# Summing the two feature halves of x2 on GpSimd ahead of the down projection's product with ones, with new stage orders on all engines

## The reference, cut to what matters

```
L0: x1 = x  + x @ W(entry) + bias(entry)             # W(entry) = U(entry) @ V, rank 30, U decoded from cond
L1: x2 = x1 + clip(((x1*style) @ weight.T)*dcoef + bias, -256, 256)
L2: w_down = down_project*dg + db                     # dg, db: one number per entry and hidden unit
    down = x2 @ w_down ; act = relu(down)
    w_up = up_project*ug + ub ; x3 = x2 + x2 + act @ w_up
L3: h, t, s = layernorms of x3 with gathered gains; m, n, r = x3 + small nets
    y = LN( silu(cat(h,t,m,n,r,s) @ W1 + b1) @ W2 + b2 ) ; out = x3 + y
```

## Time and profile before

| | |
|---|---|
| median of the runs | 519.8 us |
| span of the profiled execution, first to last instruction | 518.5 us |
| PE busy | 486.3 us, 94% |
| DVE busy | 410.5 us, 79% |
| ACT busy | 355.5 us, 69% |
| POOL busy | 406.9 us, 78% |
| DMA, mean over the span | 119 GB/s |

### The profile page before, as it was taken

The page is one execution under the profiler, slowest core; times in us unless marked ns, Lnnn a source line. Parts: engine busy times, 40 slices in busy tenths (PEclk is TensorE's granted clock), DMA queues, the critical chain, the costliest instruction groups (busy, mean ns, idle before and its releaser), DMA issues.

```text
span 518.5 us, 9615 instructions
## 1 busy us (share of the span) xinstructions
PE 486.3 (94%) x3216; PEld 361.9 (70%) x3245; DVE 410.5 (79%) x701; ACT 355.5 (69%) x666; POOL 406.9 (78%) x380
## 2 busy tenths in 40 slices
PE   8987788999999999999999999999999999988993
PEld 4854555677777686868686877777777767677782
DVE  4978697668788788788888888788888788887753
ACT  4677657558667677776878777777777776657732
POOL 6737798988798979798988888888989788786501
PEclk9999699999999999999999999999999999999997
DMA  8994507324234261708080817162534425113102
GB/s 294 336 335 98 127 1 219 82 82 127 83 89 120 60 189 36 212 21 226 0 236 11 214 33 195 53 176 72 139 110 118 133 54 148 53 40 125 41 2 80
DMA packets 35117, 61.82 MB, mean 119 GB/s; under 512 B 5107, under 2 KB 17541, under 8 KB 34708
## 3 DMA queue, kind: packets, MB, share of 16 engines
q1 hardware_dynamic: 28788, 44.01, 30.4%
q0 software_dynamic: 5440, 16.87, 11.0%
q10 hardware_dynamic: 864, 0.61, 0.4%
HBM read 52.61 MB, written 8.87 MB: 119 GB/s over the span
## 4 chain that ended last, share of the span: by engine, by line
PE 75%; ACT 7%; DVE 6%; issue 5%; POOL 5%; DMA 1%; DVEq 0%; ACTq 0%; POOLq 0%
PE ps_d L966 10%; PE ps_c L916 9%; PE ps_c L918 9%; PE ps_c L917 9%; PE ps_d L980 5%; PE ps_a L994 4%; PE ps_b L916 3%; PE ps_b L917 3%; PE ps_b L918 3%; PE ps_b L1012 3%; PE ps_a L1006 2%; POOL pw_rows L1532 2%; PE ps_a L1012 2%; DMA set_wdec<-in_W_dec 1%; PE ps_b L935 1%
## 5 line engine op out<-in xcount | busy, mean ns | idle before, releaser
L1232 ACT ACTIVATE h<-h,nb_h,rstd_h 128x256 f32<-128x256 f32 x64 | 33.3, 591 | 41.2 <-POOL nb_h L1562 41.2
L966 PE MATMUL ps_d<-xm_t,l_w 128*128 128x512 f32 x128 | 59.8, 610 | 1.7 <-DVE h L1455 0.9
L1532 POOL DMA_INDIRECT pw_rows<-in_pw,gidx x40 | 39.0, 976 | 12.2 <-issue 12.2
L1577 POOL TENSOR_TENSOR h<-xhat,pw_rows 128x1024 f32<-128x1024 f32 x16 | 38.0, 2374 | 6.4 <-ACT xhat L1232 6.4
L966 PEld LDWEIGHTS ps_d<-xm_t,l_w 128*128 128x128 f32 x128 | 23.6, 194 | 26.7 <-issue 24.5
L1596 POOL TENSOR_TENSOR w_up<-up_rep,ugub 128x1024 f32<-128x1024 f32 x16 | 38.1, 2378 | 2.9 <-DMA ugub<-ugub_scratch 1.9
L1598 POOL TENSOR_TENSOR w_up<-w_up,ugub 128x1024 f32<-128x1024 f32 x16 | 39.3, 2456 | 1.3
L1582 POOL TENSOR_TENSOR h<-h,pw_rows 128x1024 f32<-128x1024 f32 x16 | 38.3, 2396 | 1.2
L994 PE MATMUL ps_a<-act_dn,w_up 128*128 128x128 f32 x256 | 33.4, 286 | 5.3 <-ACT act_dn L1211 4.7
L1608 POOL TENSOR_TENSOR x3be<-x,ln_gb 128x1024 f32<-128x1024 f32 x16 | 37.9, 2372 | 0.3 <-DVE y_out L1513 0.3
L916 PE MATMUL ps_b<-w_h,act_t_l 128*128 128x256 f32 x128 | 37.7, 295 | 0.4 <-DVE act_t_l L1477 0.4
(11 more groups left out here) (263 smaller groups left out, 1607.9 us busy)
## 6 DMA issues: line engine op xcount, KB each, us to landing
ugub<-ugub_scratch SPq DMA_DIRECT2D x32, 512.0 KB, 6.6
x_t<-in_x_t SPq DMA_DIRECT2D x16, 512.0 KB, 6.5
out<-y_out SPq DMA_DIRECT2D x15, 512.0 KB, 7.2
set_wdec<-in_W_dec SPq DMA_DIRECT2D x2, 1920.0 KB, 9.6
set_wdec<-in_int_W SPq DMA_DIRECT2D x1, 1536.0 KB, 11.1
...
pw_rows<-in_pw,gidx POOLq DMA_INDIRECT x40, 3.6
```

The costliest lines, as they stand in the source:

```text
L966: m = eng.matmul(ps_l1[:, o, :], l1_w[:, k, o * P:(o + 1) * P], xm_t[:, k, :], start=k == 0, stop=k == KB - 1)
L1232: m = eng.activation(out[:, j, :], src[:, j, :], ACT.Identity, bias=nb[k][:, j:j + 1], scale=rstd[k][:, j:j + 1])
L1532: eng.indirect_dma_start(pw_rows[:, j, :], None, t["pw"], bass.IndirectOffsetOnAxis(ap=idx[:, j:j + 1], axis=0)).then_inc(s_pw[c.ring], 16)
L1577: eng.tensor_tensor(h1[:, :, :], xhat[:, :, :], pw_rows[:, :, 0:D], ALU.mult).then_inc(g_h1m, 1)
```

## The change

- A new tile `x2_sum` (128 x 512), a new GpSimd stage `g_xsum` that waits for x2 and for the last `pe_dn`, and writes the sum of the two feature halves of x2, and a semaphore `g_xs`.
- `pe_dn` issues four matmuls with `down_project` on x2, then waits for `g_xs`, then issues two with ones on `x2_sum`, instead of eight on x2.
- The tables of all five engines are new, in `begin`, `order` and `end`; the loop starts at another place in the cycle.
- The load of `aw` shares a semaphore with that of the biases.

```diff
+        x2_sum = late("x2_sum", [P, CH])
...
         def load_aw(eng, c):
-            eng.dma_start(aw[:, :], row(t["aw"]).broadcast_to([P, 6])).then_inc(d_aw, 16)
+            eng.dma_start(aw[:, :], row(t["aw"]).broadcast_to([P, 6])).then_inc(d_bias, 16)
...
             wait(eng, v_x2, c.n + 1)
             x = x2_t[c.ring][:, :, :].rearrange("p k (j e s) -> p k e j s", e=2, s=S)
-            for part in range(2):
-                for k in range(KB):
-                    for e in range(2):
-                        m = eng.matmul(ps_dn[e * HID:(e + 1) * HID, part * CT * S:(part + 1) * CT * S],
-                                       down_w[:, k, part * HID:(part + 1) * HID], x[:, k, e],
-                                       start=k == 0, stop=k == KB - 1)
+            for k in range(KB):
+                for e in range(2):
+                    eng.matmul(ps_dn[e * HID:(e + 1) * HID, 0:CT * S], down_w[:, k, 0:HID], x[:, k, e],
+                               start=k == 0, stop=k == KB - 1)
+            wait(eng, g_xs, c.n + 1)
+            x = x2_sum[:, :].rearrange("p (j e s) -> p e j s", e=2, s=S)
+            for e in range(2):
+                m = eng.matmul(ps_dn[e * HID:(e + 1) * HID, CT * S:2 * CT * S], down_w[:, 0, HID:P], x[:, e],
+                               start=True, stop=True)
             m.then_inc(p_dn, 1)
...
+        def g_xsum(eng, c):
+
+            wait(eng, v_x2, c.n + 1)
+            wait(eng, p_dn, c.n)
+            eng.tensor_tensor(x2_sum[:, :], x2_t[c.ring][:, 0, :], x2_t[c.ring][:, 1, :], ALU.add).then_inc(g_xs, 1)
...
-                      order=[(g_wup, 3), (g_hmul, 4), (g_hadd, 4), (g_tlow, 2), (g_rooty, 6), (g_gather, 3),
-                             (g_rooth, 4), (g_style, 2), (g_res, 4), (g_rootx, 3)],
+                      order=[(g_rootx, 3), (g_gather, 3), (g_xsum, 2), (g_wup, 2), (g_hmul, 3), (g_hadd, 3),
+                             (g_rooty, 5), (g_tlow, 1), (g_rooth, 3), (g_res, 3), (g_style, 1)],
```

More of the change, by code:

```diff
@@ L274, in conditioned_residuals @@
         x2_t = x1_t
-        (d_front, d_bdec, d_aw, d_side, d_bias, d_l1, d_wts, d_id, d_net, d_w2n, d_rown, d_w1, d_late, d_oh, d_gain, d_cls,
+        x2_sum = late("x2_sum", [P, CH])
+        (d_front, d_bdec, d_side, d_bias, d_l1, d_wts, d_id, d_net, d_w2n, d_rown, d_w1, d_late, d_oh, d_gain, d_cls,
          d_ub, d_ug, d_row) = (
             sem("d_" + n) for n in
-            "front bdec aw side bias l1 wts id net w2n rown w1 late oh gain cls ub ug row".split())
+            "front bdec side bias l1 wts id net w2n rown w1 late oh gain cls ub ug row".split())
         d_dec = [sem(f"d_dec{n}") for n in range(KB)]
@@ L314, in conditioned_residuals @@
             "x1 l1 x2 dnu dn x3t x3l bnx mvx tm tml ms msl bnh mvh h hl sill y1 y".split())
[L316 to L317 removed]
+        g_xm, g_xs, g_tl, g_vex, g_rx, g_nbx, g_h1m, g_h1, g_veh, g_rh, g_nbh, g_upm, g_up, g_x3be, g_vey, g_ry = (
+            sem("g_" + n) for n in "xm xs tl vex rx nbx h1m h1 veh rh nbh upm up x3be vey ry".split())
         x_d = t["x_t"].rearrange("(k p) (c n) -> c p k n", p=P, n=CH)
@@ L1641, in _ @@
+                      order=[(load_ub, 0), (load_ids, 2), (load_shift, 3), (load_x, 0), (store, 6), (load_up, 0)],
+                      end=[(load_shift, 13), (load_ids, 14), (load_shift, 14), (store, 10), (store, 11),
+                           (load_ids, 15), (load_shift, 15), (store, 12), (store, 13), (store, 14), (store, 15)],
                       fill=6)
@@ new lines, in _ @@
+                             (pe_warm, 4), (pe_x3r, 1), (pe_hht, 0), (pe_l1, 2), (pe_warm, 5), (pe_shift, 0),
+                             (pe_tm, 0), (pe_dn, 2), (pe_w1_x3, 0), (pe_ms, 0), (pe_xht, 1), (pe_w1_tm, 0),
+                             (pe_up, 2), (pe_cp, 1)],
+                      order=[(pe_w1_ms, 6), (pe_x1, 3), (pe_w1_h, 6), (pe_x3r, 4), (pe_t, 2), (pe_l1, 3),
+                             (pe_hht, 5), (pe_shift, 5), (pe_w1_x3, 5), (pe_tm, 5), (pe_dn, 3), (pe_w2, 6),
+                             (pe_ms, 5), (pe_xht, 4), (pe_w1_tm, 5), (pe_up, 3), (pe_cp, 4)],
```

211 lines of the change are left out of this document (97 added, 114 removed).

## The result

The change makes the kernel slower: 544.38 us (median of 4 runs, 544.15 to 545.02) against 520.42 us of the kernel before beside it (517.51 to 522.46), a ratio of 1.0481, with a 95% interval of [1.0449, 1.0512]. The forecast was 530.5 us. The profiled execution took 544.18 us, its span is 542.2. Medians and ratios here leave out the one run that fell in a slower state (602.1 us, of vector_sum_new_tables).

The account below looks back on a forecast made before the run. PE was taken to bound the kernel before; nine intervals at 28.4 - 27.21 add 10.7 us, neighbouring intervals 0.4, drain -0.5: +10.6 on the 518.5 us span, 529.1, plus 1.3 to the median, 530.5 us. The 8-in-10 range was 516 to 538.

Parts of the forecast that it names:

- PE bounds the kernel before, 0.47 us saved.: Down projection on PE: PE alone sets the chunk's length; two of eight matmuls go, 0.47 us a chunk.
- The sum takes 1.26 us.: New 128x512 sum on POOL: 1.26 us, from a row of the same shape and engine.
- The wait closes a loop of 28.3 to 28.4 us.: POOL's wait for x2 delays the next style product, hence the next x2; interval at least 28.3, taken as 28.4 us.
- the signs: Expected in the changed profile: PE waits about 1 us for `xm_t` each chunk; no other POOL idle over 1 us.
- the two loops: Steady loop: one through the style product and L1 product, one through the root and gather; both 28.3 us.
- The other moves ... 0 (bounds 0 and 0.3 us a chunk).: Reordering on PE and ACT only swaps work within one engine: 0, bounds 0 and 0.3 us a chunk.
- The decode and the chain through the first chunk stand as they did. I take 0, with 2 us either way.: Setup: W1 and the nets land later, the first chunk's loads earlier; 0, with 2 us either way.
- 0.2 each, 0.4 together: Intervals ahead of and behind the nine: already 28.2 us, so each gains only 0.2 us, together 0.4.
- -0.5 for the last down projection: Drain: the last down projection saves 0.5 us.
- That the kernel speeds up: Rival for the loop: PE stays the bound, POOL's late start absorbed; 26.74 to 26.9 us an interval, 513 us; chance 0.2.
- Only POOL's own loop holds: Rival of no change: DVE never stands for h, loop through POOL alone 27.56 us, 522.5 us total; chance 0.17.
- The port in full: Shared-port rival: `x_t_l` meets `x3be` rather than the root; 29.9 us an interval, 547 us; chance 0.06.

Follow-up runs that it names:

- vector_sum_new_tables: Changed kernel with the sum made on VectorE right behind the addition that makes x2, not on GpSimd; 548.2 us, ratio 1.058 to the kernel before.
- half_ones: Kernel before with two matmuls left out, the ones product over one feature half of x2 only, no sum, result not the reference's; 514.4 us, ratio 0.991.
- no_sum_act_back: Changed kernel without the sum, with PE's and GpSimd's old cycles, early small nets, and th2 ahead of tm's high half on ACT; 529.4 us, ratio 1.019.
- nets_early: Changed kernel with the small nets' load moved right behind the side matrix's load in the setup DMA queue; 537.8 us, ratio 1.036 to the kernel before.
- late_ones: Tables of before, GpSimd sum behind the up weights for chunks 3 to 14 only, PE work ahead of the two sum matmuls; 529.2 us, ratio 1.019.
- vector_sum_old_tables: Tables of before, six matmuls on PE, and the sum on VectorE right behind the addition that makes x2; 529.9 us, ratio 1.020.

## Why the forecast fell short

**PE bounds the kernel before, 0.47 us saved.** Right: 0.45 measured (half_ones).

**The sum takes 1.26 us.** Right: 1.27 to 1.29.

**The wait closes a loop of 28.3 to 28.4 us.** Right in place and within 0.1 in length: 28.47. Counted from the start of the sum at 271.54, h is ready at 10.9 us (10.9 forecast), `x_t_l` starts at 14.4 (14.4), x1 is ready at 18.1 (18.1), the L1 product starts at 20.3 (20.3), the root of x at 21.4 (21.3), and the next sum at 28.5 (28.3). Of its parts, DVE's stop ahead of the statistics of h was 1.19 us for 1.5, the gap ahead of the gather 0.58 to 0.65 for 0.55, `x_t_l` 1.22 as said. PE's lost time is 28.47 - 26.77 = 1.70 for the 1.6 forecast; only 0.9 of it shows as waits (0.52 and 0.38), the rest I have not traced. Two of the signs were off: PE waits 0.5 us for `xm_t`, not 1, and POOL idles 1.09 to 1.19 us ahead of the root of x, where I had said nothing over 1 us. Of the two loops the one through the gather is the longer, since the sum starts behind the last indirect DMA and 0.37 to 0.40 us after x2.

**"The other moves ... 0 (bounds 0 and 0.3 us a chunk)."** Wrong for the tables by themselves: 0.57 us an interval, twice the bound, and half of it is th2 on ACT (0.32, no_sum_act_back). In the changed kernel I find nothing of it in the loop: DVE's wait for the squares of y is 0.28 us there and lies ahead of the stop for h, which swallows it. It is why taking the sum away gives back only 0.69 of the 1.26 us between the two kernels.

**"The decode and the chain through the first chunk stand as they did. I take 0, with 2 us either way."** This is the step that failed. I saw that the nets land later and did not follow them to who waits: 3.86 us of PE, then the lower clock through the first L1 product, 8.25 us at dn 0 and 5.65 at dn 2. Given how dn 2 varies, the loss is 3.5 to 5.65 us; nets_early takes all of it back.

**"0.2 each, 0.4 together" for the intervals outside the nine.** Failed too. The loop is closed as soon as there is a sum to wait for. From dn 2 to dn 4 the changed kernel loses 3.4 us and without the sum only 0.9, so 2.5 us there are the sum, 1.25 a chunk. In the drain 3.0 are lost and 1.5 without the sum, where I had -0.5 for the last down projection. With 3.2 and 3.3 us more than forecast these two stretches weigh as much as the setup, and neither failed step explains the miss without the other.

In the terms of the sum: 10.7 forecast and 11.6 measured for the nine intervals, 0 and 5.65 for the setup, 0.2 and 3.4 ahead of the loop, -0.3 and 3.0 behind it. Of the 13.1 us missing, 0.9 lie where I looked hardest.

**The rivals.** That the kernel speeds up needed POOL's late start to be absorbed; in late_ones it was not, even with PE's wait covered. "Only POOL's own loop holds" asked that DVE should not stand for h, and it does, 1.19 us a chunk. The port in full did not happen in the loop: `x_t_l` kept its 1.22 us. The other side of the meeting is one that I hadn't priced: the root's last operation begins while `x_t_l` runs and takes 0.73 us in place of 0.20.

```profile
286.47 0.73 POOL L1566 TENSOR_TENSOR nb_h<-nm_h,rstd_h 128x4 f32<-128x4 f32 x1
```

It cost nothing here, since POOL then still waits 0.25 us for x1; in late_ones the same kind of meeting lies in the loop.

No version here with a true sum beats the kernel before; the nearest, late_ones and vector_sum_old_tables, are 2% slower. The reason that the runs suggest: half_ones shows at least 0.45 us of room in every loop but PE's, and the sum costs 1.27 us on one engine and 0.69 to 1.30 on the other. On either engine, in the places tried, it made some loop longer than PE's work, 28.02 or 27.54 us.
